# Moving products between waits, and storing rows in halves, in a fused two-layer mixture-of-experts kernel on one core

## The reference

```python
x = x + ffn0(cond0(x, itok7, L0_cond_weights, fside), ...)   # layer 0
x = x + ffn1(cond1(x, W, A, Bm, scalings, itok6), ...)       # layer 1
# cond0: per sequence a 32x32 matrix, picked by itok7, over its 32 rows, plus a bias
# ffn0:  scores = softmax(xt @ gate_w.T); the two best of 8 experts, inner width 176
#        y = sum of weight_e * (silu(xt @ w1[e].T) * (xt @ w3[e].T)) @ w2[e].T
#        z = (silu(xt @ sw1.T) * (xt @ sw3.T)) @ sw2.T        # shared, inner width 352
# cond1: x @ W.T + scaling * (x @ A_b.T) @ B_b.T              # rank 16, picked by itok6
# ffn1:  gelu(q(x) @ q(wg0)) * (q(x) @ q(wg1)), then q(.) @ q(w_linear)   # 8-bit floats, hidden 1024
```

## Time and profile before

| | us |
|---|---|
| median of 3 executions | 422.24 |
| all three | 422.24, 420.89, 422.67 |
| the profiled execution's own time | 422.06 |
| its span, from first to last instruction | 420.2 |
| TensorE busy | 407.9 |
| VectorE, ScalarE, GpSimd busy | 312.7, 249.1, 191.5 |

### The profile page before, as it was taken

The page is one execution under the profiler, slowest core; times in us unless marked ns, Lnnn a source line. Parts: engine busy times, 40 slices in busy tenths (PEclk is TensorE's granted clock), DMA queues, the critical chain, the costliest instruction groups (busy, mean ns, idle before and its releaser), DMA issues.

```text
span 420.2 us, 8696 instructions
## 1 busy us (share of the span) xinstructions
PE 407.9 (97%) x2956; PEld 332.7 (79%) x2956; DVE 312.7 (74%) x732; ACT 249.1 (59%) x552; POOL 191.5 (46%) x195
## 2 busy tenths in 40 slices
PE   7899999999999999999999999999999999999994
PEld 6467788888899999999999998875575755757663
DVE  6987999997976766666666655769778787787853
ACT  3996566475356666556555644337558475484763
POOL 3320079701764454445445005637567575575011
PEclk9999999999999999999999999999999999999999
DMA  7999300000365555466465422312232243231102
GB/s 229 376 369 367 96 0 2 1 2 11 96 197 158 168 167 166 147 181 162 145 182 153 124 76 78 87 50 77 88 89 91 60 126 91 87 94 57 51 2 101
DMA packets 37258, 50.44 MB, mean 120 GB/s; under 512 B 4472, under 2 KB 30464, under 8 KB 37216
## 3 DMA queue, kind: packets, MB, share of 16 engines
q1 hardware_dynamic: 30288, 32.15, 22.7%
q0 software_dynamic: 6480, 17.70, 15.7%
q10 hardware_dynamic: 448, 0.03, 0.1%
HBM read 32.18 MB, written 17.69 MB: 119 GB/s over the span
## 4 chain that ended last, share of the span: by engine, by line
PE 83%; DVE 10%; ACT 4%; issue 1%; DMA 1%; DVEq 0%; ACTq 0%
PE bank L1165 17%; PE bank L1167 16%; PE bank L1166 16%; PE bank L1439 13%; PE bank L1454 6%; PE bank L1328 4%; PE bank L1367 2%; PE bank L1366 2%; PE bank L1348 2%; PE bank L1405 2%; ACT xtr L476 1%; DVE hsl L790 1%; DVE hsf L783 1%; PE bank L1187 1%; ACT xtT L490 1%
## 5 line engine op out<-in xcount | busy, mean ns | idle before, releaser
L412 POOL DMA_INDIRECT xg<-kept,perm x71 | 68.6, 966 | 82.9 <-PE bank L1328 50.0
L1439 PE MATMUL bank<-h,wg 128*128 128x512 fp8e4 x256 | 62.0, 381 | 0.2 <-ACT ff L656 0.2
L419 POOL DMA_INDIRECT ga<-slots_out,slot x32 | 32.8, 1025 | 37.3 <-SPq L357 21.2
L1165 PE MATMUL bank<-w13h,xgl 128*128 x142 | 48.9, 344 | 0.1
L991 DVE TENSOR_TENSOR hrl<-bank,hrh 128x256 fp32r<-128x256 f32 (+1 forms) x36 | 15.2, 421 | 44.3 <-ACT hrh L595 44.3
L1439 PEld LDWEIGHTS bank<-h,wg 128*128 128x128 fp8e4 x256 | 22.6, 98 | 31.5 <-ACT ff L656 12.5
L1167 PE MATMUL bank<-w13h,xgh 128*128 x142 | 45.6, 321 | 0.0
L1166 PE MATMUL bank<-w13l,xgh 128*128 x142 | 45.6, 321 | 0.0
L654 ACT ACTIVATE gel<-bank 128x512 bf16<-128x512 f32 x64 | 39.7, 620 | 6.7 <-PE bank L1439 3.5
L419 POOL DMA_INDIRECT gb<-slots_out,slot x32 | 37.6, 1174 | 9.8 <-issue 9.8
L401 POOL TENSOR_SCALAR places<-cst,placef 128x72 f16<-128x72 f32 x28 | 26.1, 950 | 31.8 <-DVE placef L878 31.8
(11 more groups left out here) (198 smaller groups left out, 1164.4 us busy)
## 6 DMA issues: line engine op xcount, KB each, us to landing
slots_out<-yr SPq DMA_DIRECT2D x35, 256.0 KB, 2.1
xres<-in_x SPq DMA_DIRECT2D x8, 512.0 KB, 9.8
kept<-xtr SPq DMA_DIRECT2D x7, 512.0 KB, 8.9
out_x<-fin SPq DMA_DIRECT2D x7, 512.0 KB, 2.8
w13raw<-in_rw SPq DMA_DIRECT2D x8, 352.0 KB, 5.0
w2raw<-in_rw SPq DMA_DIRECT2D x8, 256.0 KB, 6.5
wgst<-in_wgate SPq DMA_DIRECT2D x16, 128.0 KB, 2.6
xg<-kept,perm POOLq DMA_INDIRECT x71
```

The costliest lines, as they stand in the source:

```text
L412: pool.indirect_dma_start(out=xg[i % GATHERS][:, j, :], out_offset=None, in_=kept, in_offset=bass.IndirectOffsetOnAxis(perm[:, 2 * i + j:2 ...
L419: pool.indirect_dma_start(out=buf[:, g % 2, j, :], out_offset=None, in_=slots_out, in_offset=bass.IndirectOffsetOnAxis(slot[:, k, g * GT + ...
L1165: pe.matmul(dst, al, bh, start=first, stop=False, skip_group_check=True)
L1439: ins = pe.matmul(bank[bk][:, :], wg8[:, kk, half, c * P:(c + 1) * P], h8[:, k, kk, :], start=(kk == 0), stop=(kk == KC - 1))
```

## The change

TensorE's order: `ranks()` comes one up part later. In groups 1 to 3 the first two chunks of `shared_down(i)` no longer stand together: `shared_up(i + 1)`'s first part stands between them. The end: the last but one group's second half is added by VectorE, not by GpSimd, and its rows are stored as two transfers of 256 KB. The first stage: group 0's x comes in two halves, the second issued by ScalarE; router 6 and the first `logits` stand ahead of the first up part, VectorE's first `shifted` ahead of `shared_x_lo(1)`; there are nine `ones` fewer (33, 4 and 11 for 37, 6 and 14).

```diff
-            sp.dma_start(xres[:, 0:GT, :], x_t[0]).then_inc(x_in[0], 16)
+            sp.dma_start(xres[:, 0:2, :], x_t[0][:, 0:2, :]).then_inc(x_first[0], 16)
...
-            for g in range(GROUPS - 1):
+            for g in range(GROUPS - 2):
                 sp.wait_ge(s("fin_ready"), g * 2 + 2)
                 sp.dma_start(out_t[g], fin[:, g % 2]).then_inc(o_out[g % 2], 16)
+            sp.wait_ge(s("fin_ready"), 2 * GROUPS - 3)
+            sp.dma_start(out_t[GROUPS - 2][:, 0:2, :], fin[:, 0, 0:2, :]).then_inc(o_out[0], 16)
+            sp.wait_ge(s("half_ready"), 1)
+            sp.dma_start(out_t[GROUPS - 2][:, 2:GT, :], fin[:, 0, 2:GT, :]).then_inc(o_out[0], 16)
...
-                for h in range(2):
+                for h in range(2 if g < GROUPS - 2 else 1):
                     pool.wait_ge(s("ob_ready"), g * 2 + h + 1)
-                    if g == GROUPS - 2 and h:
-                        pool.wait_ge(s("act8_ready"), GROUPS * HC)
...
             act.dma_start(pick[:, :], pick_in).then_inc(s("pick_in"), 16)
+            act.dma_start(xres[:, 2:GT, :], x_t[0][:, 2:GT, :]).then_inc(x_first[1], 16)
...
+            shifted(0)
             shared_x_lo(1)
             routed_weight_lo(0)
-            shifted(0)
...
             ffn(GROUPS - 1, 1, False, True)
+            dve.wait_ge(s("ob_ready"), 2 * GROUPS - 2)
+            dve.wait_ge(o_out[0], 16 * (GROUPS // 2 - 1))
+            dve.tensor_tensor(fin[:, 0, 2:GT, :].rearrange("p a b -> p (a b)"), xm[:, 0, 2:GT, :].rearrange("p a b -> p (a b)"),
+                              ob[:, 2:GT, :].rearrange("p a b -> p (a b)"), ALU.add).then_inc(s("half_ready"), 1)
...
-            ones(WARM + WARM // 2 + 4)
+            ones(WARM + WARM // 2)
...
-            ones(6)
+            ones(4)
             condition(0)
-            ones(WARM // 2 + 3)
+            ones(WARM // 2)
...
+                if i == GROUPS - 2:
+                    logits(0)
...
+            router(GROUPS - 2)
             pe.wait_ge(s("sw_split"), KC)
-            pe.wait_ge(s("xt_ready"), TILES - 3)
             shared_up(0, True, parts=[0])
             transpose_xt(GROUPS - 1)
-            router(GROUPS - 2)
-            logits(0)
...
             shared_down(0, first=True, chunks=[2])
+            shared_up(1, parts=[2])
             ranks()
             for i in range(1, EARLY - 2):
-                shared_up(i, parts=range(2, 6))
-                shared_down(i, chunks=range(2))
-                shared_up(i + 1, parts=range(2))
+                shared_up(i, parts=range(3 if i == 1 else 2, 6))
+                shared_down(i, chunks=[0])
+                shared_up(i + 1, parts=[0])
+                shared_down(i, chunks=[1])
+                shared_up(i + 1, parts=[1])
                 shared_down(i, chunks=[2])
```

More of the change, by code:

```diff
@@ L276, in adaln_ffn @@
                      "comb_a comb_done xm_T xm_hi xm_split xa_done xa_m xa_hi xa_split H_done h8_ready "
-                     "gate_done up2_done gel_ready ff1_ready act_ready act8_ready down_done act8_used ob_ready fin_ready last_ready").split():
+                     "gate_done up2_done gel_ready ff1_ready act_ready act8_ready down_done act8_used ob_ready fin_ready half_ready last_ready").split():
             s(name)
+        x_first = [sem(f"x_first{h}") for h in range(2)]
         x_in = [sem(f"x_in{g}") for g in range(GROUPS)]
@@ L364, in _ @@
                 sp.dma_start(out_t[GROUPS - 1][:, j0:j1, :], fin[:, 1, j0:j1, :]).then_inc(o_out[1], 16)
-            sp.wait_ge(o_out[0], 16 * GROUPS // 2)
+            sp.wait_ge(o_out[0], 16 * (GROUPS // 2 + 1))
             sp.wait_ge(o_out[1], 16 * (GROUPS // 2 - 1 + len(LAST)))
@@ L669, in last_out @@
                 for n, (j0, j1, b) in enumerate(LAST):
-                    act.wait_ge(s("fin_ready"), g * 2 - 1 if n == 0 else g * 2)
+                    if n == 0:
+                        act.wait_ge(s("fin_ready"), g * 2 - 1)
+                    else:
+                        act.wait_ge(s("half_ready"), 1)
                     act.wait_ge(s("down_done"), g * 2 + n + 1)
@@ L1170, in condition @@
                 pe.wait_ge(s("rows_ready"), i + 1)
-                pe.wait_ge(x_in[i], 16)
+                for sem_in in x_first if i == 0 else [x_in[i]]:
+                    pe.wait_ge(sem_in, 16)
                 for b in range(BPT):
```

## The result

The changed kernel takes 420.99 us (median of 20 executions, 419.75 to 421.86) against 421.77 for the kernel before (20 executions). The ratio is 0.9964, with a 95% interval of 0.9946 to 0.9982: 1.5 us faster, 0.8 to 2.3. The ratio goes with the means (422.40 and 420.93 us); the medians lie only 0.8 us apart, since the kernel before has more late executions. I had forecast 422.1 us and no change. The time lies in the range; the direction was missed. Of all the executions behind this document three, at 505.77, 575.03 and 577.0 us with a granted clock of 0.75 or less, are left out of the ratios.

The account below looks back on a forecast made before the run. TensorE, busy 97% of the span, was taken to bound the kernel. Terms +0.1 (first stage), 0 (ranks, down 1.1), +0.75 (up 4.0), -0.9 (end) sum to -0.05 us: forecast 422.1 us, no change, range 420.6 to 423.6.

Parts of the forecast that it names:

- The end: Last rows stored in halves, VectorE adding the second: last piece lands and is issued sooner, -0.9 us (bounds 0.4 to 1.2).
- the last piece stands in a queue: At the end, 512 KB stores delay the last 128 KB piece: 2.9 us to land; without the queue 2.1 or less.
- The first stage: Kernel start: x halves, router and logits order, nine `ones` fewer; -0.7 to +0.6 us at VectorE's row of 35.52, taken +0.1.
- I cost the halves at nothing: First stage: splitting x gains zero, since TensorE stands 1.16 us before the next group's products at 9.15 anyway.
- the stall at 14.76: First stage: TensorE's 0.65 us issue stall, read as late code, moves into transposes 2, ending between 15.8 and 16.7 us.
- the rival at 420.7: Code blocks come in time, first stage gains both stalls, 0.65 + 0.60 us; whole kernel 420.7 us; chance 0.08.
- The clock rival: Fewer `ones` let the clock rise later: first stage's products take twice as long, +2.2 to +2.5 us a group; 424.5; chance 0.09.
- my own sign of being wrong: First stage: the prediction fails if a row of `ones` x11 lasts over a microsecond.
- Ranks, down 1.1 and up 2.0: TensorE near 46.9 and 54 us: removed waits (0.5 us at ranks, about 0.2 at down 1.1) are waited out: 0.
- The wait near 54: TensorE's wait before the second chunk of `shared_down(1)`, old start 54.55 us: forecast down to a half.
- Up 4.0: First part of `shared_up(4)`, near 80 us: TensorE waits about 1.5 us for VectorE's `xtL`; +0.75 us (bounds 0, +1.05).
- The 0.27 us of slack at down 4.1: Second chunk of `shared_down(4)` starts at 92.94 though TensorE is ready at 92.67; this swallows 0.27 of 1.05 us delay.

Follow-up runs that it names:

- first_alone: Kernel before with the first stage's part of the change alone; ratio 0.9984 (0.9962 to 1.0006), 0.7 us faster.
- ones_back: Changed end and first stage with the old order between them, but 37, 6 and 14 `ones` again; ratio to the kernel before 0.9939 (0.9918 to 0.996).
- tail_first: Kernel before with the changed end and first stage, old order of ranks, down chunks and up parts between them; ratio 0.9939, median 419.89 us.
- gpsimd_late: Changed kernel with one tiny fill (8 values a partition) added at the end of GpSimd's program; ratio to the kernel before 0.9983 (0.996 to 1.0006).
- halves_gpsimd: Kernel before with the last but one group's rows stored in two transfers, GpSimd still adding the second half; ratio 0.9981 (0.9961 to 1.0001).
- order_alone: Kernel before with only the new order of ranks, down chunks and up parts; ratio 1.0005 (0.9983 to 1.0027).
- keep_i3: Changed kernel, but for i = 3 the old order (both down chunks, then both up parts); ratio to the kernel before 0.9942, median 420.04 us.

## Why the prediction was wrong, point by point

**The end, forecast -0.9 us.** The direction was right, the size half of the 1.79 us measured, and the step behind it wrong: "the last piece stands in a queue ... With the queue gone the last piece lands in 2.1 us or less". The queue was there and did go (2.9 to 1.9 us), but it didn't set the end. GpSimd did, 5.6 us behind its addition. I read the earlier trace rows up to the last landing and never asked why the span ends 1.09 us behind it. Measured in column k: 1.35 us for taking the addition from GpSimd, 0.12 for the halves, 0.32 more in all kernels with both the new end and the x halves, together 1.79. In all ten traces with x halves the third copy on ScalarE comes 0.36 or 0.37 us behind the start of TensorE's last product, in all six without 0.64 or 0.65. With the halves ScalarE's program has one recorded instruction more (707 for 706), and the 0.2 us called issue ahead of that copy is gone. That it is a matter of where the code lies is only argued.

**The first stage, forecast +0.1 us.** The step "I cost the halves at nothing: TensorE stands 1.16 us in front of the next group's products at 9.15 anyway" failed. The earlier trace rows lays that wait on `wrow`, which was done at 8.83. The products started at 9.15 because their x landed at 9.10, by an issue that had stood in SyncE's queue. The wait was no cover but the thing itself. The products of that group start at 9.35 in the mean of the six traces without halves and at 8.96 in the ten with them, and VectorE's row of 35.52, without the two latest, at 35.25 and 34.83. That is 0.4 us; the timings give 0.7 (first_alone), with an interval that holds zero. Which of the stage's edits the rest belongs to is open. The Trainium skill, Trainium Kernel Development and Optimization, Key Constraints, says that DMAs issued from several engines share the same 16 DMA engines. The runs don't disagree with that. But by its saving nothing but issue time the prediction kept a zero, and that is not what the traces show: the split changed which transfer came first, and the second group's x landed at 7.4 to 8.8 us in place of 8.4 to 10.0.

**Code stalls and clock.** I had forecast the stall at 14.76 moved; it is not in the changed kernel's trace. It goes with the number of `ones`: all seven traces with 37, 6 and 14 have it (0.14 to 1.77 us), none of the nine with 33, 4 and 11. Why is not shown; that TensorE comes to that place of its program later with the clock up later would fit. The stalls' absence is what the rival at 420.7 asked for, but ones_back, where one of 0.41 us came back, takes the same time, so its gain of 1.25 us was not there.

The clock rival's condition did come, and with it my own sign of being wrong: the eleven `ones` take 1.35 us, the pace of 1.2 GHz as in the first 33, and so do the transposes at 9.95 (1.97 us, 1.09 before). Its price of 2.2 to 2.5 us a group isn't seen in the timing (ones_back and tail_first both 0.9939, each within about 0.3%) nor in most traces. One trace shows a price: in gpsimd_late TensorE was busy 0.49 us of the two from 5 to 7, and its windows of 9 to 18 us read

```profile
9.00:11.00 2.00, 2.00 (x33) 0.81 (x34) 1.97 (x2) 1.71 (x5) 1.40 (x3) 0.54 1.10 379
11.00:13.00 2.00, 2.00 (x24) 1.62 (x39) 1.93 (x3) 1.01 (x3) 0.00 (x0) 0.50 1.06 412
13.00:16.00 3.00, 3.00 (x48) 1.89 (x20) 2.93 (x3) 2.67 (x7) 0.00 (x0) 0.50 1.04 371
16.00:18.00 2.00, 2.00 (x56) 1.29 (x48) 1.93 (x3) 1.57 (x5) 1.96 (x2) 1.00 1.10 348
```

The column behind GpSimd's is the granted clock: half of full speed until 16 us. The second group's transposes, at 13.84 us, still take 1.90 us there, the chain passes to ScalarE's copies at 17.07 us, not at 15.64 as in the changed kernel, and VectorE's row stands at 36.40, 1.45 us later than there. So fewer `ones` cost about 1.4 us in one trace of nine; in the other eight column c stands 25.55 to 26.15 us behind b, with more `ones` 25.56 to 26.33 (without halves_gpsimd).

Elsewhere a slow start is covered: from 15.64 us on the chain runs over ScalarE's copies, as its shares by line from 13 to 29 us in the changed kernel show, 76.9% in the three rows of `xtr` and `xtT`:

```profile
by line: ACT xtr L480 37.3%; ACT xtT L494 30.5%; ACT xtr_last L480 9.1%; PE bank L1199 8.9%; PE bank L1209 7.6%; PE bank L1189 3.8%; PE bank L1176 2.6%; ACT lraw L498 1.0%; issue 0.4%
```

**Ranks, down 1.1 and up 2.0, forecast 0.** Right: 79.69 without them, 79.75 with them. The wait near 54 didn't halve; TensorE's idle there went from 0.22 to 0.52 us (0.50 to 0.80 from start to start). Counted from column c, TensorE comes there 0.46 us earlier, about what the ranks' wait had cost, and goes on 0.16 us earlier.

**Up 4.0, forecast +0.75 us.** Right in mechanism and size. Wait 1.64 us (forecast about 1.5); start 1.33 us behind that of `xtL` (forecast 1.29); column e +0.76 us in order_alone. The 0.27 us of slack at down 4.1 were swallowed as said: its wait is gone.

**The sum.** By the runs: -0.4 to -1.0 (stage), 0 (ranks), +0.75 (up 4.0), -1.8 (end), so -1.4 to -2.1 us; -1.5 was measured. The rival that came nearest in time, without code stalls at 420.7, did so by luck: it had the end at -0.9.

## What to carry to other kernels

Look at what lies between the last landing and the end of the span: if it is more than a few tenths of a microsecond, find the engine that finishes late, and give GpSimd nothing in the last six microseconds that another engine has a gap for. A wait laid on an operation that was done long before is a wait for something else, often a DMA; read the landing before you count such idle time as cover. And before moving a product ahead, look up where its operand is made on the other engine: here one exchange of three gave back about a third of what the rest had won, and leaving that exchange out takes it back. Moving that operation takes the wait away, though the timing doesn't show a gain.

## What the runs showed of the hardware

GpSimd's DRAIN ends 5.55 to 5.57 us behind its last operation in all traces, be it an addition of 1.15 us or a fill of 0.13 us; the DRAIN of ScalarE takes 0.39 us beside a copy of 0.38 us, that of SyncE 7 ns.

The routed stretch of TensorE (36 pairs) takes 132.25 to 132.30 us in eleven traces and 133.12 or 133.13 in five, spread evenly: the median from a third product to the next first one is 0.161 in place of 0.156 us, at a granted clock of 1.00 in both kinds. One program showed both. What sets it is open.

With 37, 6 and 14 `ones` the first group's eight transposes start 0.117 us apart in all seven traces; with 33, 4 and 11 they start 0.221 us apart in seven of nine. In three of these nine (tail_first, keep_i3, gpsimd_late) the granted clock fell to 0.50 at 7.7, 8.8 and 9.2 us and came back to 1.00 at 11.1, 12.2 and 16.0 us.
